# A new order of the steps on all five engines, in a recurrent layer with experts, on one core

## What is computed

```python
x = x + rwkv(layernorm(x))        # block 1
x = x + experts(layernorm(x))     # block 2
x = x + recurrence(layernorm(x))  # block 3
x = x + experts(layernorm(x))     # block 4

# block 1: time mix, then channel mix
k, v, r = mix(xn) @ w_key, mix(xn) @ w_value, mix(xn) @ w_recept
x = x + wkv(exp(decay), first, k, v) * sigmoid(r) @ w_output   # wkv: a weighted running mean over time
fk, fr = mix(xn2) @ f_w_key, mix(xn2) @ f_w_recept
x = x + sigmoid(fr) * (square(relu(fk)) @ f_w_value)

# block 3: h_t = a_t * h_{t-1} + sqrt(1 - a_t^2) * i_t * conv(x)_t, with a_t and i_t from two gates
out = h @ W_out.T;  out = out * rsqrt(mean(out^2)) * gamma
```

## Time and profile before

| | us |
|---|---|
| three runs, median | 1257.09 |
| lowest and highest of them | 1254.84 and 1258.42 |
| span of the profiled execution | 1254.1 |
| PE busy in it | 1186.7 |
| DVE busy | 886.8 |
| ACT busy | 699.7 |
| POOL busy | 537.4 |

### The profile page before, as it was taken

The page is one execution under the profiler, slowest core; times in us unless marked ns, Lnnn a source line. Parts: engine busy times, 40 slices in busy tenths (PEclk is TensorE's granted clock), DMA queues, the critical chain, the costliest instruction groups (busy, mean ns, idle before and its releaser), DMA issues. The chain is left out here.

```text
span 1254.1 us, 17087 instructions
## 1 busy us (share of the span) xinstructions
PE 1186.7 (95%) x5812; PEld 927.7 (74%) x5812; DVE 886.8 (71%) x1508; ACT 699.7 (56%) x1100; POOL 537.4 (43%) x514
## 2 busy tenths in 40 slices
PE   5699999999999999999999989999999999999982
PEld 2377787887776868778786768778778678688871
DVE  7989886757587757677889898678567655654336
ACT  2464463555554637455568677567676464554633
POOL 3537652435153062443478637436353602253024
PEclk9799999999999999999999999999999999999997
DMA  7012154646458267575331045657555554656534
GB/s 211 17 34 51 13 164 134 186 122 191 158 138 240 73 162 212 157 202 163 92 85 34 1 105 154 186 158 180 139 146 159 167 167 144 198 140 200 141 100 127
DMA packets 113030, 170.78 MB, mean 136 GB/s; under 512 B 10024, under 2 KB 86576, under 8 KB 112944
## 3 DMA queue, kind: packets, MB, share of 16 engines
q1 hardware_dynamic: 94864, 124.59, 31.2%
q0 software_dynamic: 12320, 39.86, 16.0%
q10 hardware_dynamic: 5760, 5.25, 1.2%
HBM read 138.20 MB, written 16.27 MB: 123 GB/s over the span
## 5 line engine op out<-in xcount | busy, mean ns | idle before, releaser
L2248 PE MATMUL psum<-fwv,hid 128*128 128x256 f32 x1024 | 239.9, 380 | 2.6 <-ACT hid L1225 2.6
L786 POOL TENSOR_TENSOR rstd<-varis,half_neg 128x4 f32<-128x4 f32 x64 | 101.2, 1580 | 282.4 <-DVE varis L3169 191.8
L2248 PEld LDWEIGHTS psum<-fwv,hid 128*128 128x128 f32 x1024 | 190.0, 190 | 32.6 <-issue 4.6
L2289 PEld LDWEIGHTS psum<-xst,ew 128*128 128x128 f32 x1024 | 123.9, 192 | 7.5 <-issue 3.1
L2289 PE MATMUL psum<-xst,ew 128*128 128x128 f32 x1024 | 124.8, 275 | 0.5 <-ACT xst L1306 0.5
L1319 ACT ACTIVATE hidt<-psum 128x512 f32<-128x512 f32 x80 | 47.7, 597 | 133.4 <-PE psum L2289 118.1
L2297 PE MATMUL psum<-ew,hidt 128*128 128x256 f32 x512 | 116.0, 379 | 2.6 <-DMA ew<-in_w 1.9
L1221 ACT ACTIVATE hid<-psum 128x512 f32<-128x512 f32 x128 | 75.5, 593 | 62.4 <-PE psum L2169 40.5
L2297 PEld LDWEIGHTS psum<-ew,hidt 128*128 128x128 f32 x512 | 96.5, 190 | 18.6 <-ACT hidt L1319 2.9
L790 POOL TENSOR_SCALAR xhat<-rows_ring,negmean,rstd 128x256 f32<-128x256 f32 x108 | 96.5, 903 | 24.6 <-PE psum L2158 17.9
L2169 PE MATMUL psum<-xfk_hi,fwk_hi 128*128 128x512 f32 x256 | 93.7, 447 | 1.8 <-issue 1.8
(11 more groups left out here) (303 smaller groups left out, 2496.3 us busy)
## 6 DMA issues: line engine op xcount, KB each, us to landing
ew<-in_w SPq DMA_DIRECT2D x64, 1024.0 KB
ew<-in_w SPq DMA_DIRECT2D x64, 512.0 KB
rows_ring<-bias_rows POOLq DMA_DIRECT2D x28, 512.0 KB, 5.6
rows_ring<-in_x SPq DMA_DIRECT2D x14, 512.0 KB, 6.2
rows_ring<-y POOLq DMA_DIRECT2D x14, 512.0 KB, 5.6
out<-rows_ring SPq DMA_DIRECT2D x14, 512.0 KB, 6.5
rows_ring<-space POOLq DMA_DIRECT2D x12, 512.0 KB
ys_rows<-ys ACTq DMA_DIRECT2D x40, 128.0 KB
```

The lines of the kernel that those rows point to most:

```text
L786: pool.tensor_tensor(dst, src, half_neg[:, 0:src.shape[1]], ALU.pow).then_inc(done, 1)
L2248: last = nc.tensor.matmul(rows4[:, k, :], hid[:, j % NHID, k * P:(k + 1) * P], fwv[:, j, :], start=j == 0 and k % 2 == 0, stop=j == FC - 1 ...
L2289: last = nc.tensor.matmul(bank_e[:, j * P:(j + 1) * P], ew1[:, c, at:at + P], xst[:, c, :], start=c == 0, stop=c == DC - 1)
```

## The change

All five lists of step calls are written in another order. The steps are the same ones, with the same arguments: 130 on SP, 187 on POOL, 708 lines on PE, 542 on DVE. On ACT the steps are the same too, but they stand in an order that needs the other function table more often, so `preload_act_table_set` stands there 16 times more: 91 table loads run where 75 did (8 more of each table). The helpers that make the instructions are not touched.

The diff is 3600 lines of moved calls. Four pieces of it, from PE, DVE, SP and ACT:

```diff
@@ PE, turn_16
                 channel_value(15, 6)
-                tile_up(38, 0)
                 channel_value(15, 7)
-                freed(fr_out, 15, "s")
+                tile_up(38, 1)
+                freed(fr_out, 15, 's')
                 rec_products(14)
-                tile_up(38, 1)
                 tile_down(38)
...
@@ PE, turn_14
                 two_up(29, 0)
                 channel_value(13, 0)
-                freed(ev2, 13, "e1")
-                freed(fin, 11, f"f{TC - 1}")
-                transposes_rec(12)
                 two_up(29, 1)
+                channel_key(13, 1)
+                two_turn(29, 0)
                 channel_key(13, 2)
                 channel_key(13, 3)
-                two_turn(29, 0)
+                two_turn(29, 1)
+                freed(ev2, 13, 'e1')
+                freed(fin, 11, f'f{TC - 1}')
+                transposes_rec(12)
                 channel_key(13, 4)
-                two_turn(29, 1)
                 channel_value(13, 1)
                 two_down(29)
...
@@ DVE, turn_9 and turn_10
             def turn_9():
+                stats_in(10)
                 second_differences(8)
                 channel_mix_key(8)
                 channel_mix_receptance(8)
-                stats_in(10)
...
             def turn_10():
+                stats_in(11)
                 recur(5)
                 channel_mix_low(9)
+                gated_values(8)
                 weights_decayed(10)
-                stats_in(11)
+                combine(8)
                 mean_square(5)
                 weights_now(10)
                 finish(5)
                 beta_sums(10)
-                gated_values(8)
...
@@ SP, turn_16
             def turn_16():
-                store(13)
-                load_first(38)
-                load_second(38)
+                store(10)
                 load_first(39)
+                store(12)
                 load_second(39)
                 store(14)
+                store(13)
                 store(15)
```

More of the change, by code:

```diff
@@ L623, in turn_8 @@
                 store(4)
+                store(3)
+                load_x(11)
             def turn_9():
@@ L2508, in turn_4 @@
                 receptances(3)
-                gate_products(0, [(relu, 3, f"f{j}") for j in (2, 3, 4)])
                 tile_up(4, 0)
+                gate_products(0, [(relu, 3, f'f{j}') for j in (2, 3, 4)])
+                channel_value(3, 2)
+                tile_up(4, 1)
+                freed(fr_out, 3, 's')
+                transposes_in(5)
                 channel_key(3, 5, 0)
-                tile_up(4, 1)
+                tile_down(4)
                 channel_key(3, 6, 0)
-                channel_value(3, 2)
@@ L2655, in turn_7 @@
-                freed(ev3, 3, "c1")
+                tile_in(14)
+                freed(ev3, 3, 'c1')
                 receptances(6)
-                channel_value(6, 1)
-                two_down(13)
-                freed(fr_out, 6, "s")
+                tile_up(14, 0)
+                channel_value(6, 2)
+                tile_up(14, 1)
+                gate_products(3, [(relu, 6, f'f{j}') for j in (2, 3, 4)])
+                freed(fr_out, 6, 's')
                 transposes_in(8)
-                tile_in(14)
@@ L2662, in turn_7 @@
-                gate_products(3, [(relu, 6, f"f{j}") for j in (2, 3, 4)])
-                tile_up(14, 0)
+                tile_down(14)
                 channel_key(6, 5, 3)
-                tile_up(14, 1)
+                channel_value(6, 3)
+                tile_in(15)
                 channel_key(6, 6, 3)
-                tile_down(14)
-                channel_value(6, 2)
                 channel_key(6, 7, 3)
-                tile_in(15)
-                freed(ev1, 8, "e1")
+                channel_value(6, 4)
@@ L2945, in turn_13 @@
-                freed(ev3, 11, "c1")
-                outputs(13)
-                gate_products(11, [(relu, 12, f"f{j}") for j in (7, 5, 6)])
+                gate_products(11, [(relu, 12, f'f{j}') for j in (7, 5, 6)])
+                keys(14)
+                tile_down(27)
+                freed(zsum, 13, 'z')
+                transposes_mid(13)
                 channel_value(12, 6)
-                tile_up(27, 1)
+                tile_in(28)
                 channel_value(12, 7)
-                freed(zsum, 13, "z")
@@ L3076, in turn_16 @@
+                freed(fin, 13, f'f{TC - 1}')
+                transposes_rec(14)
+                tile_up(37, 0)
+                channel_key(15, 4)
+                channel_value(15, 1)
                 tile_up(37, 1)
-                channel_key(15, 4)
+                channel_value(15, 2)
                 tile_down(37)
-                channel_value(15, 1)
-                gate_products(14, [(relu, 15, f"f{j}") for j in (2, 3, 4)])
+                gate_products(14, [(relu, 15, f'f{j}') for j in (2, 3, 4)])
```

2075 lines of the change are left out of this document (1041 added, 1034 removed).

## The result

| kernel | us, median | ratio to before | 95% interval |
|---|---|---|---|
| before | 1256.4 | 1 | |
| changed | 1286.4 | 1.0236 | 1.022 to 1.0251 |
| forecast | 1252.8 (1247.0 to 1260.5) | 0.997 | |

The changed kernel loses 30 us where 4 were to be gained. The spans of the two profiled executions, 1254.1 and 1282.4 us, differ by 28.3. The expectations call PE, DVE, ACT, POOL and SP by their long names: TensorE, VectorE, ScalarE, GpSimd and SyncE.)

What follows compares the result with a forecast made beforehand. PE, busy 1186.7 of 1254.1 us, was taken as the bound, with DVE setting the pace from 650 to 750 us. Gains of 5.25 us less 1 us of new waits took 1257.09 to 1252.8 us, range 1247.0 to 1260.5.

Steps and rivals of the forecast that it cites:

- Place one: Near 143 us: PE's wait for ACT's square between channel_key(1,7) and channel_value(1,7) goes, -0.95 us.
- Place three: At 1008 us: the wait of two_down(29)'s second half for weights goes, -2.2 us, at worst nothing.
- Place four: The tail: tile_down(38) no longer starts late for ACT's gelu, as rec_products(14) stands between, -0.7 us.
- for certain: Said in the nothing-arrives rival (chance 0.21): near 143 us and in the tail, 1.65 us together are sure gains.
- The head: Start of the kernel: earlier statistics of batch 1 against later ACT weight preparation, taken as 0, with 1.5 us either side.
- The sum: Whole kernel: gains of 0.95 + 1.4 + 2.2 + 0.7 = 5.25 us, before 1 us set against them.
- place two: DVE, 599 to 733 us: batch 10's statistics fill idle time, so gate_products(7) starts earlier, -1.4 us (0 to 2.31).
- I put it at nothing: Cost of stats_in(11), gated_values(8) and combine(8) preceding finish(5) on DVE: at most one 2.31 us step, taken as nothing.
- the new waits: Anywhere in the kernel: small waits dealt out again by the new order, 1 us lost, bounds 0 and 4.
- The rival on the slow side: ACT's 16 extra table loads, half hitting waited-for places: 10.2 us lost less 5.25 gained, 1262.0 us, chance 0.16.
- the sign that was named for it: At channel_value steps close behind their channel_key: PE's waits for ACT grow from 2.6 us to several.
- the longer wait for weights of tile 39: Sign of a wrong forecast: a longer weight wait before the last recurrence, as SP has a store between its two loads.

Runs made afterwards that it cites:

- before_two_moves: The kernel before with only two TensorE steps moved, channel_key(1,7) ahead of outputs(2) and two_down(29) behind receptances(13): ratio 0.9982, 1254.6 us.
- before_to_13: The changed kernel with the order of before put back on all five engines to the end of turn 13, changed order in turns 14 to 16: ratio 0.9984.
- before_late_rows: The kernel before with VectorE's experts_rows(1) of turn 11 moved behind combine(9), weights_decayed(11), weights_now(11) and third_stats(8): ratio 1.0084, 10.5 us slower.

## Why the prediction was wrong

**The gains: places one and three right in mechanism.** Place one came: PE reached keys(3) at 144.20 us instead of 146.28, with no wait for ACT (and lost it all at transposes_mid(2) behind it); 0.6 of these 2.1 us it had at the start of the turn already. Place three came. This is two_down(29) after, answering, all 32 matmuls in one row and no wait:

```profile
1037.36 3.67 PE L2345 MATMUL psum<-ew,hidt 128*64 128x256 f32 x32
```

Place four came in kind, for tile_down(38) no longer waits for gelu, but no time came with it. From rec_products(14) or tile_up(38, 1), whichever stands first, to the end of the span it is 59.0 us before and 59.1 after. PE's waits on this way add up to 16.0 us for 16.8, with 2.0 for 1.2 at gate_products(15), and rec_products(15), behind the last wait, takes 6.70 us for 5.40. So "for certain" was too strong for this place. The head was put at 0 and came 0.8 us shorter (keys(1) at 48.86 us instead of 49.70): the two waits of the head changed places, as shown above. The sum was 3.85 us with place two left out; before_two_moves, with places one and three (3.15 in the forecast), measured 2.3, and before_to_13, with three and four (2.9), 2.0.

**Place two: did not arrive.** gate_products(7) starts at 753.66 us, after a wait of 1.02, not at 731. The statistics of batch 10 were said to need only rows of x. In the changed kernel they wait 2.00 us for a step of POOL (line 790, writing y):

```profile
611.37 1.40 DVE L3178 BATCH_NORM_STATS2 stats<-rows_ring 128x6 f32<-128x256 f32 x4 [2.00 <-POOL y L790]
```

That step ends at 611.26 us, and second_differences(8) follows at 613.69 without a wait: the 5.99 us of idle time, which were to be filled, are not there any more. Ahead of the statistics stands recur(4), now the last step of turn 8, which waits 5.27 us for POOL's scaled input. From second_differences(8) to gate_products(7) it is 134.4 us before and 140.0 after. What lengthened it, the picking, the merges or POOL's queue, was not taken apart. "I put it at nothing", said of the DVE steps moved ahead, was too small as well: stats_in(11) stands ahead of recur(5) from 690.76 to 693.58 us, and both rec_products(5) and transposes_rec(6) wait there, 5.5 and 1.8 us where it was 0.7 and 0.2.

**The step that failed: the new waits, 1 us with bounds 0 and 4.** They are some 33 us (29.7 lost, and about 3 of the gains in it), and in the profiled spans about a third of the loss is not waiting but matmuls at a lower clock behind the waits, which the sum had no term for. The reason given, that a new order deals out small waits again of the size of those removed, took the size from a list in which the kernel's close places do not show, because there the waits are hidden. The rows hold only what is late now. What can become late is the work that is just in time: norm2(2), which ended at 146.19 us, 3.5 us ahead of transposes_mid(2) at 149.71, behind 25 us of scatters; gather(20), whose tile_in(20) followed 7.8 us after its issue with no wait, where before_late_rows shows 6.2 us from issue to tile_in, so 1.6 us of slack. The forecast followed the PE-to-PE distances, and for POOL only one chain near 720 us. It did not follow the routing, the copies or the experts' rows, though the order of the steps shows each of their moves.

**The rival on the slow side** named another engine, ACT, with 5 us lost; PE's waits for ACT add up to 5.6 us in the changed kernel and 6.7 in the kernel before, so the sign that was named for it is missing. So is the longer wait for weights of tile 39: tile_down(39) waits 1.1 us, for gelu, where it waited 1.9 for weights. The other sign named for a wrong forecast is there: the loss from 650 to 750 us is 11.9 us of PE's time, above 6.

## To carry to other kernels

Five in-order lists were changed together here, and the loss did not come from the waits that the profile shows but from steps that had no wait and little slack. So list, for each list that issues transfers, what stands behind a transfer that must land first, and for each chain over three or more engines (here routing, and rows stored and gathered back) how early it was. In this kernel a fitting order was a property of all lists at once. Undoing one step or chain in the new order gave 3 to 4 us, hardly told from zero; moving one in the old order cost up to 10.8 us. The routing was tried both ways: 4 us came back in the new order, where the experts' rows were as late, and 10.8 us were lost in the old one. To find where time went, put back whole stages on all engines; to find how, move one step alone in the kernel that fits, exactly as far as the change moves it.

## What the runs showed of the hardware

**TensorE's clock after a wait.** After the 7.20 us at transposes_mid(2) in the changed kernel the granted clock is at half, which is 1.2 GHz of 2.4, for 4.5 us, and then comes back (columns of the stretches as above):

```profile
140.00:147.00 7.00, 7.00 (x28) 5.02 (x27) 5.67 (x15) 0.60 (x1) 5.47 (x6) 1.00 0.02 0
...
155.00:159.50 4.50, 4.50 (x12) 2.95 (x13) 1.04 (x1) 1.45 (x2) 3.49 (x6) 0.50 0.30 2
159.50:163.00 3.50, 3.50 (x9) 1.50 (x9) 3.26 (x5) 1.71 (x3) 2.75 (x2) 0.96 0.58 101
```

From its start to the next step's, transposes_mid(2) there takes 1.73 us for 0.88 and value_columns(3) 4.94 for 3.43, so a wait of 7.2 us costs 9.6. before_late_rows shows the same behind its 9.06 us: 0.50 from 768 to 772 us, 1.00 from 774.

**A transfer that adds into rows, issued by GpSimd,** of 512 KB, held the queue for 5.00 and 5.15 us, and what depends on it went 6.0 and 6.1 us after its issue. The Trainium skill (DMA: Bandwidth & Descriptors, Anatomy of one DMA, SWDGE path) fits 2.0 us plus the bytes by 436 thousand per us, an estimate of 3.2 us here. The rows show nearly twice that, and so does the page of the profile: for the 28 transfers of this size that read bias_rows its median from issue to landing is 5.6 us before the change and 6.0 after. Other traffic does not explain it in the changed kernel: from 652 to 659 us its DMA engines moved 75 GB/s, 0.53 MB in all, hardly more than this one transfer.
